# A four-layer kernel with post-norms: in the third layer 22 tiles of x are turned by the DMA as 16-bit planes, and ScalarE parts the planes of the first layer's pairs

## The chip, the cores and the metric

The kernel runs on one core of a Trainium2 chip. The metric is the time of one launch in microseconds on the device, as the median of several runs. The engines are TensorE (PE), VectorE (DVE), ScalarE (ACT), GpSimd (POOL) and SyncE (SP), which here only issues transfers.

## The reference

x has 4 batches of 1024 tokens with 1024 features. Four blocks follow one another, each with a residual and a layer norm:

```python
x = _layernorm(x + x @ (W0 * blockmask).T)                      # first layer
x = _layernorm(x + x @ W1.T + bias + lora_of_batch(x))          # second layer
x = _layernorm(x + mixer(x))     # to 128 features, 4 x (scan, MLP), back to 1024
x = _layernorm(x + x @ W.T + b + routed_lora(x))                # third layer
```

In the last line the router takes the mean of x over tokens 179 to 1022 of a batch, a softmax over 8 experts, and adds the experts' low-rank products with these weights. So the weights of a batch are only known when all its tiles have come out of the mixer.

## The kernel before

All work goes by tiles of 128 tokens, 32 for a layer, 8 for a batch. The counter s runs through the three dense layers: 0 to 31 the first, 32 to 63 (A_END, B_END) the second, 64 to 95 the third. A dense product has the weights as the wide operand and x, with the features on the partitions, as the narrow one. Both are split into a high part (fp32r) and the rest, and three matmuls of 128x512 are made for each of 8 chunks and 2 halves: lines 885 to 887, 48 matmuls a tile. ScalarE makes the high part of x (`split_x`, line 1370), VectorE the low one (line 1824).

**First layer.** Tiles 7 to 26 go in ten pairs (a, a+1), each by seven products of half size (A11, A12, S2, S3, S1, S4, A22, lines 964 to 966, 12 matmuls each). A11, S2 and S1 accumulate in bank 0, and ScalarE copies it out after each (`hold` 0, 1, 2, line 1391). The sums of x that S1 to S4 take are made by VectorE (`add_x`, lines 1872 to 1879). VectorE joins a bank with a held part into the rows of the output (`join`, line 1894): join 1 reads S3's bank and hold 2, and A22 must wait for it. The order of each engine is written out by hand. For pair p+1 the operands are made while pair p is multiplied.

A finished row is normalised in place by ScalarE (`normalise`, lines 1411 and 1414, after GpSimd's root, line 2625). The second layer needs it with the features on the partitions. In the first layer GpSimd therefore copies its lower and its upper 16 bits into two planes (`part_planes`, line 2636, one buffer), ScalarE's queue stores them (`send_planes`, line 1422), SyncE's queue reads them back with a transposing DMA (line 632), and GpSimd joins the planes to 32-bit words (`join_planes`, line 2643).

**Third layer.** Its input comes from the mixer's readout: for tile c of the mixer TensorE makes 6 matmuls (`read_out`), VectorE adds the residual and takes statistics (`residual`, lines 2231 to 2243), GpSimd the root (`root_c`, line 2685), ScalarE normalises in place (`normalise_c`, line 1553) and stores the tile to `x3` (line 1557). VectorE and GpSimd add it to the batch's total (`add_up`). Here these tiles are called mix tiles. They lie in three places (`cx`). The mix tiles of batch b+1 are made during the steps of batch b; tiles 8 and 9 before. C_STEP says in which: steps 0 to 3 of batches 1 and 2, two tiles each; the first of a step is added in that step, the second at the start of the next. After step 4 (SUM_STEP; 5 in batch 0) TensorE reduces the total (`reduce_total`), and in steps 6 and 7 it makes 16 weight parts for the next batch, with VectorE, ScalarE and GpSimd (`weight_lo`, line 2650); SyncE loads them.

x of step s is loaded as it is (`load_x`, line 639, two places), turned on TensorE at the start of step s-1 by 8 transposes (`turn_x`, line 897), and split from PSUM. SyncE's queue holds the loads of x, of the mixer's output, of the mix tiles and of the weights in one order, and a wait there holds back what stands behind it. The load of a mix tile (`load_c`, line 681) waits until the tile before it in its place has been stored and added up.

## Time and profile before

| | us |
|---|---|
| median of 3 runs | 1653.36 |
| lowest, highest | 1652.39, 1657.66 |
| the profiled execution | 1656.23 |
| its span, first to last instruction | 1654.3 |
| TensorE busy | 1614.8 (98%) |
| VectorE, ScalarE, GpSimd busy | 1175.0, 666.4, 618.5 |
| TensorE's granted clock, mean | 0.988 |

The profiled execution is 2.9 us above the median, 1.9 us of it lie outside its span. Matmuls overlap: one of 128x512 shows 0.39 us, but they start 0.227 us apart. The pairs run from 94 to 306 us, the second layer from 370 to 816 us, the mixer to about 1160 us, the third layer to the end.

### The profile page before, as it was taken

What the parts mean: (1) busy time and instruction counts of PE and PEld (TensorE: products, weight loads), DVE (VectorE), ACT (ScalarE), POOL (GpSimd) and SP (SyncE); (2) the same over time, 40 slices, a digit from 0 to 9 for tenths busy, and PEclk for the clock granted to TensorE, in tenths of its full rate; (3) what the DMA queues carried; (4) which work ended last, traced back from release to release, by engine and by line L of the source; (5) the groups of instructions that cost most, each with busy time, mean ns of one, the idle gap of its engine ahead of it and who ended that gap; (6) DMA issues with size and microseconds to landing.
All of it is one profiled execution on the core that took longest, in us unless ns stands there. A gap on an engine that the chain in (4) does not pass through costs nothing.

```text
span 1654.3 us, 22809 instructions
## 1 busy us (share of the span) xinstructions
PE 1614.8 (98%) x7734; PEld 1299.1 (79%) x7734; DVE 1175.0 (71%) x2150; ACT 666.4 (40%) x987; POOL 618.5 (37%) x507
## 2 busy tenths in 40 slices
PE   8999999999999999999999999999899999999998
PEld 7877777788888888888866666676788788888886
DVE  6978888566666666568878777778767776676633
ACT  3544443443333333323345555545433333343311
POOL 4323333353333323213577777762213222221200
PEclk9999999999999999999999999999899999999999
DMA  7233333555444444543140000003546555555321
GB/s 281 78 114 102 121 102 102 183 144 131 118 120 120 119 114 125 152 113 77 46 158 27 1 1 1 1 13 115 203 147 214 193 196 188 181 203 182 138 79 51
DMA packets 140195, 196.58 MB, mean 119 GB/s; under 512 B 75954, under 2 KB 84146, under 8 KB 139826
## 3 DMA queue, kind: packets, MB, share of 16 engines
q1 hardware_dynamic: 115250, 125.92, 26.3%
q10 hardware_dynamic: 24832, 69.22, 11.0%
q8 instruction: 63, 1.03, 0.3%
q14 instruction: 50, 0.41, 0.1%
HBM read 105.97 MB, written 72.35 MB: 108 GB/s over the span
## 4 chain that ended last, share of the span: by engine, by line
PE 78%; DVE 10%; issue 5%; ACT 3%; DMA 2%; POOL 1%; ACTq 0%; SPq 0%; DVEq 0%; POOLq 0%
PE ps L885 15%; PE ps L887 14%; PE ps L886 14%; PE ps L1131 7%; PE ps L1073 3%; PE ps L1031 2%; PE ps L1079 2%; PE ps L1123 2%; PE ps L964 2%; PE ps L1121 2%; PE ps L1122 2%; PE ps L897 2%; PE ps L966 2%; PE ps L965 2%; PE ps L1099 1%
## 5 line engine op out<-in xcount | busy, mean ns | idle before, releaser
L2625 POOL TENSOR_TENSOR rstd<-var_eps,minus_half 128x1 f32<-128x1 f32 x96 | 89.8, 936 | 556.9 <-DVE minus_mean L1909 556.9
L885 PE MATMUL ps<-wall_x,x_hi 128*128 128x512 f32 x688 | 273.8, 398 | 4.9 <-ACT wall_x L1476 2.1
L887 PE MATMUL ps<-wall_x,x_lo 128*128 128x512 f32 x688 | 268.9, 391 | 0.0
L886 PE MATMUL ps<-wall_x,x_hi 128*128 128x512 f32 x688 | 268.8, 391 | 0.0
L885 PE MATMUL ps<-wall_y,x_hi 128*128 128x512 f32 x512 | 201.9, 394 | 0.0
L886 PE MATMUL ps<-wall_y,x_hi 128*128 128x512 f32 x512 | 199.4, 389 | 0.0
L887 PE MATMUL ps<-wall_y,x_lo 128*128 128x512 f32 x512 | 199.4, 389 | 0.0
L885 PEld LDWEIGHTS ps<-wall_x,x_hi 128*128 128x128 f32 x688 | 129.6, 188 | 34.5 <-ACT wall_x L1476 4.4
L887 PEld LDWEIGHTS ps<-wall_x,x_lo 128*128 128x128 f32 x688 | 129.5, 188 | 27.8
L886 PEld LDWEIGHTS ps<-wall_x,x_hi 128*128 128x128 f32 x688 | 129.7, 189 | 25.2
L1841 DVE TENSOR_TENSOR row<-ps,bias 128x512 f32<-128x512 f32 x128 | 87.8, 686 | 86.8 <-PE ps L887 85.5
L1542 ACT ACTIVATE g<-ps,b 128x512 f32<-128x512 f32 x128 | 83.8, 679 | 123.8 <-PE ps L1123 123.3
L1131 PE MATMUL ps<-g,w 128*128 128x512 f32 x256 | 127.1, 619 | 0.0
L1844 DVE BATCH_NORM_STATS2 stats<-row 128x6 f32<-128x512 f32 x152 | 105.1, 694 | 26.2 <-ACT row L1404 21.8
L1414 ACT ACTIVATE row<-row,shift,rstd 128x1024 f32<-128x1024 f32 x96 | 119.5, 1245 | 3.2
L1411 ACT ACTIVATE shift<-minus_mean,rstd 128x1 f32<-128x1 f32 x96 | 28.0, 292 | 223.0 <-POOL rstd L2625 222.9
L887 PEld LDWEIGHTS ps<-wall_y,x_lo 128*128 128x128 f32 x512 | 96.1, 188 | 20.4
L886 PEld LDWEIGHTS ps<-wall_y,x_hi 128*128 128x128 f32 x512 | 96.2, 188 | 18.9
L885 PEld LDWEIGHTS ps<-wall_y,x_hi 128*128 128x128 f32 x512 | 96.2, 188 | 18.8
L2643 POOL COPY x_in<-x_planes 128x1024 uint16<-128x1024 uint16 x64 | 86.3, 1395 | 29.1 <-DMA x_planes<-x_scratch 26.1
L1370 ACT ACTIVATE x_hi<-ps 128x1024 fp32r<-128x1024 f32 x32 | 32.7, 1023 | 151.1 <-PE ps L897 148.1
L2636 POOL COPY planes_early<-row 128x1024 uint16<-128x1024 uint16 x54 | 65.9, 1249 | 61.2 <-ACT row L1414 48.1
(329 smaller groups left out, 3633.9 us busy)
## 6 DMA issues: line engine op xcount, KB each, us to landing
x_scratch<-row ACTq DMA_DIRECT2D x32, 512.0 KB, 2.7
x_in<-x_scratch SPq DMA_DIRECT2D x32, 512.0 KB, 4.0
out<-row ACTq DMA_DIRECT2D x32, 512.0 KB, 2.8
x_in<-in_x_t SPq DMA_DIRECT2D x29, 512.0 KB, 3.8
w_first<-in_w_t SPq DMA_DIRECT2D x56, 256.0 KB, 2.9
x_scratch<-planes_early ACTq DMA_DIRECT2D x27, 512.0 KB, 3.3
cx<-x_scratch SPq DMA_DIRECT2D x24, 512.0 KB, 4.3
x_scratch<-cx ACTq DMA_DIRECT2D x24, 512.0 KB, 3.6
```

What stands on the lines that cost most here:

```text
L885: pe.matmul(bank, hi[:, k], wall[:, k, 0, cols], start=(k == 0), stop=False)
L886: pe.matmul(bank, hi[:, k], wall[:, k, 1, cols], start=False, stop=False)
L887: return pe.matmul(bank, lo[:, k], wall[:, k, 0, cols], start=False, stop=(k == KC - 1))
L1073: last = pe.matmul(ps[:, bank, c:c + 1], squares[:, c * P:(c + 1) * P], mean_col[:], start=True, stop=True)
L1131: pe.matmul(ps[:, OUT], w2[:, FCH * (n // UNITS) + i], g[:, i], start=(i == 0), stop=(i == FCH - 1)).then_inc(o_done, 1)
L1414: act.activation(row[:, i], row[:, i], ACT.Identity, bias=shift[:, i:i + 1], scale=rstd[:, i:i + 1])\
L1542: act.activation(g[:, i], ps[:, F0 + i % 2], ACT.Silu, bias=of_layer(b1[:, :, i], n))\
L1841: dve.tensor_tensor(row[:, i, cols], ps[:, out_bank(s, half)], bias[:, cols], ALU.add)\
L1844: mark(dve.bn_stats(stats[:, i, half], row[:, i, cols]))
L2625: pool.tensor_tensor(rstd[:, i:i + 1], var_eps[:, i:i + 1], minus_half[:, 0:1], ALU.pow)\
L2636: pool.tensor_copy(planes[s >= S_END][:, part], halves[:, part]).then_inc(parted, 1)
L2643: pool.tensor_copy(halves[:, part], x_planes[:, part].rearrange("p k t -> p (k t)"))\
```

## The change

- **Third layer.** From mix tile 10 on (`C_PLANES`), that is from step 74 (`PLANES_FROM`), the tiles go by planes. ScalarE parts a normalised mix tile into two planes (`part_c`, 2 activations) and issues two stores instead of one. The planes go to two places that alternate (`c_planes`), one of them with its second half in a place of its own. SyncE issues two transposing DMAs for the step two ahead, instead of a plain load for the step three ahead. GpSimd joins them (`join_planes(s + 2)`, behind the roots and sums of the step), and x is split from SBUF. TensorE turns only tiles 64 to 73.
- **The places of mix tiles.** `load_c` waits until the tile before it is parted, not until it is stored.
- **Pairs.** The planes of tiles 7 to 24 and of tile 6 are parted by ScalarE, not GpSimd. ScalarE's order in a pair changes: parting of a-2, `normalise(a - 1)` and A12's high part come ahead of hold 1, the parting of a-1 behind it.

```diff
@@ turn_count, c_stores and new helpers
+C_PLANES = TPB + 2
+PLANES_FROM = B_END + C_PLANES
+def c_norm_count(c):
+    return c + 1 + 2 * max(0, c - C_PLANES)
@@ load_x
-                if s - 2 >= B_END:
+                if s > PLANES_FROM:
+                    sp.wait_ge(x_turned, turn_count(s - 1))
+                elif s - 2 >= B_END:
                     sp.wait_ge(x_turned, turn_count(s - 2))
...
-                    sp.wait_ge(c_stored[c_slot(c)], 16 * c_uses(c))
+                    sp.wait_ge(c_stored[c_slot(c)], c_stores(c))
+                    if s >= PLANES_FROM:
+                        for part in range(2):
+                            sp.dma_start_transpose(x_planes[:, part], x3_planes[c - C_PLANES, part])\
+                              .then_inc(x_loaded[0], 16)
+                        return
@@ load_c
-                    sp.wait_ge(c_stored[slot], 16 * c_uses(last))
+                    if last < C_PLANES:
+                        sp.wait_ge(c_stored[slot], c_stores(last))
+                    else:
+                        sp.wait_ge(c_normed, c_norm_count(last) + 2)
@@ SyncE, steps of the third layer
-                    load_x(s + 3)
+                    if s + 3 < PLANES_FROM:
+                        load_x(s + 3)
+                    if s + 2 >= PLANES_FROM:
+                        load_x(s + 2)
@@ TensorE, steps of the third layer
-                    if s + 1 < D_END:
+                    if s + 1 < PLANES_FROM:
                         turn_x(s + 1)
@@ ScalarE, new functions
+            def part_planes(s):
+                halves = row[:, s % 2].bitcast(U16).rearrange("p (f h) -> p h f", h=2)
+                act.wait_ge(normed, norm_count(s))
+                act.wait_ge(stored[(s - 1) % 2], 16 * ((s - 1) // 2 + 1))
+                for part in range(2):
+                    act.activation(planes[0][:, part], halves[:, part], ACT.Identity).then_inc(parted, 1)
+                send_planes(s)
+            def part_c(c):
+                act.wait_ge(c_normed, c_norm_count(c))
+                at_least(act, c_stored[c_slot(c)], c_stores(c) - 32)
+                if c >= C_PLANES + 2:
+                    act.wait_ge(c_stored[c_slot(c - 2)], c_stores(c - 2))
+                halves = c_place(c).bitcast(U16).rearrange("p (f h) -> p h f", h=2)
+                for part in range(2):
+                    act.activation(c_planes[c % 2][part][:], halves[:, part], ACT.Identity).then_inc(c_normed, 1)
+                act.wait_ge(c_normed, c_norm_count(c) + 2)
+                for part in range(2):
+                    act.dma_start(x3_planes[c - C_PLANES, part], c_planes[c % 2][part][:])\
+                       .then_inc(c_stored[c_slot(c)], 16)
@@ ScalarE, pairs
                 if p > 0:
-                    send_planes(a - 2)
-                hold(p, 1)
+                    part_planes(a - 2)
                 normalise(a - 1)
                 if more:
                     op_hi(p + 1, A12)
                 else:
                     split_x(S_END)
+                hold(p, 1)
+                part_planes(a - 1)
...
-                send_planes(a - 1)
@@ ScalarE, steps of the third layer
-                    for i in C_STEP[b].get(j - 1, ()):
-                        normalise_c(c + i)
+                    late = C_STEP[b].get(j - 1, ())
+                    if late:
+                        normalise_c(c + late[0])
+                        part_c(c + late[0])
+                        normalise_c(c + late[1])
+                        part_c(c + late[1])
@@ GpSimd, pairs
-                if p > 0:
-                    part_planes(a - 2)
                 root(a - 1)
-                part_planes(a - 1)
@@ GpSimd, steps of the third layer
+                    if PLANES_FROM <= s + 2 < D_END:
+                        join_planes(s + 2)
                     for i in PART_STEP[b].get(j, ()):
```

**ScalarE in a pair of the first layer**, before. `held` is hold 0 and then hold 1; `x_in_125` is tile a+1, `x_in_126` the next pair's first tile:

```order
L1384 ACTIVATE x_hi<-x_in_125 128x512
L1391 ACTIVATE held<-ps 128x512
L1384 ACTIVATE x_hi<-x_in_126 128x512
L1422 DMA x_scratch<-planes_early 128x2x1024
L1391 ACTIVATE held<-ps 128x512
L1411 ACTIVATE shift<-minus_mean,rstd 128x1
L1414 ACTIVATE row<-row,shift,rstd 128x1024
L1384 ACTIVATE x_hi<-x_in_126 128x512
L1384 ACTIVATE sum_hi<-x_sum 128x512 x2
```

And with the change:

```order
L1417 ACTIVATE x_hi<-x_in_125 128x512
L1424 ACTIVATE held<-ps 128x512
L1417 ACTIVATE x_hi<-x_in_126 128x512
L1458 ACTIVATE planes_early<-row 128x1024 x2
L1463 DMA x_scratch<-planes_early 128x2x1024
L1444 ACTIVATE shift<-minus_mean,rstd 128x1
L1447 ACTIVATE row<-row,shift,rstd 128x1024
L1417 ACTIVATE x_hi<-x_in_126 128x512
L1424 ACTIVATE held<-ps 128x512
L1458 ACTIVATE planes_early<-row 128x1024 x2
L1463 DMA x_scratch<-planes_early 128x2x1024
L1417 ACTIVATE sum_hi<-x_sum 128x512 x2
```

Two partings have come in, and A12's high part (the second `x_in_126`) stands ahead of the second `held` instead of behind it.

**SyncE around the start of step 3 of batch 1**, before: two mix tiles, then x, then the mixer's output of the next mix tile:

```order
L681 DMA cx_146<-x_scratch 128x1024
L681 DMA cx_147<-x_scratch 128x1024
L639 DMA x_in_126<-x_scratch 128x1024
L691 DMA cz<-z_hi_scratch 128x128
L691 DMA cz<-z_lo_scratch 128x128
```

And with the change:

```order
L711 DMA cx_146<-x_scratch 128x1024
L711 DMA cx_147<-x_scratch 128x1024
L663 DMA_TRANSPOSE x_planes<-x_planes 128x8x128 x2
L721 DMA cz<-z_hi_scratch 128x128
L721 DMA cz<-z_lo_scratch 128x128
```

The two transposes stand where the load of x stood, but for the step after the next.

**GpSimd in step 2 of batch 1**, before, from the root of the last step's row:

```order
L2625 TENSOR_TENSOR rstd<-var_eps,minus_half 128x1
L2703 TENSOR_TENSOR total<-cx_147,total 128x512
L2685 TENSOR_TENSOR c_rstd<-c_var_eps,minus_half 128x1
L2703 TENSOR_TENSOR total<-cx_145,total 128x512
L2685 TENSOR_TENSOR c_rstd<-c_var_eps,minus_half 128x1
```

And with the change:

```order
L2684 TENSOR_TENSOR rstd<-var_eps,minus_half 128x1
L2765 TENSOR_TENSOR total<-cx_147,total 128x512
L2747 TENSOR_TENSOR c_rstd<-c_var_eps,minus_half 128x1
L2765 TENSOR_TENSOR total<-cx_145,total 128x512
L2747 TENSOR_TENSOR c_rstd<-c_var_eps,minus_half 128x1
L2704 COPY x_in_126<-x_planes 128x1024 x2
```

The join has come in behind the root of the step's first new mix tile.

## Rows read from the trace of the kernel before

**Rows 1.** The page, part 1: busy time of the engines.
```profile
PE 1614.8 (98%) x7734; PEld 1299.1 (79%) x7734; DVE 1175.0 (71%) x2150; ACT 666.4 (40%) x987; POOL 618.5 (37%) x507
```

**Rows 2.** TensorE's waits, whole span: us in total, times, longest.
```profile
PE ps L964 <- DVE row L1894: 12.1, 9, 2.3
```

**Rows 3.** Stretches: us, busy PE, PEld, DVE, ACT, POOL, clock, DMA share, GB/s.
```profile
94.00:306.00 212.00, 198.26 (x858) 160.62 (x857) 171.75 (x394) 91.03 (x149) 66.12 (x62) 0.99 0.33 108
410.00:700.00 290.00, 289.86 (x1485) 246.54 (x1484) 182.94 (x294) 105.91 (x159) 85.40 (x63) 1.00 0.48 125
1331.00:1436.00 105.00, 105.00 (x515) 87.39 (x514) 76.25 (x152) 40.87 (x56) 26.00 (x27) 1.00 0.59 198
```

**Rows 4.** Timeline of ScalarE in a pair: start us, us, instruction, idle before.
```profile
167.54 0.60 ACT L1391 ACTIVATE held<-ps 128x512 f32<-128x512 f32 x1 [4.01 <-PE ps L966]
...
169.50 0.61 ACT L1384 ACTIVATE x_hi<-x_in 128x512 fp32r<-128x512 f32 x1
```

**Rows 5.** Timeline of VectorE in the same pair.
```profile
170.15 1.09 DVE L1851 TENSOR_TENSOR x_lo<-x_in,x_hi 128x512 fp32r<-128x512 f32 x1 [2.68 <-ACT x_hi L1384]
171.16 1.52 DVE L1872 TENSOR_TENSOR x_sum<-x_in 128x512 f32<-128x512 f32 x1
...
174.53 1.28 DVE L1851 TENSOR_TENSOR sum_lo<-x_sum,sum_hi 128x512 fp32r<-128x512 f32 x2
175.74 0.68 DVE L1894 TENSOR_TENSOR row<-ps,held 128x512 f32<-128x512 f32 x1
```

**Rows 6.** Timeline of GpSimd in the same pair: a root, two copies of planes.
```profile
165.56 0.98 POOL L2625 TENSOR_TENSOR rstd<-var_eps,minus_half 128x1 f32<-128x1 f32 x1 [0.22 <-DVE minus_mean L1909]
169.66 2.48 POOL L2636 COPY planes_early<-row 128x1024 uint16<-128x1024 uint16 x2 [3.12 <-ACT row L1414]
```

**Rows 7.** Timeline of TensorE from S4 to A22 of that pair.
```profile
175.27 0.39 PE L966 MATMUL ps<-wall_x,sum_lo 128*128 128x512 f32 x1
176.57 0.47 PE L964 MATMUL ps<-wall_y,x_hi 128*128 128x512 f32 x1 [0.91 <-DVE row L1894]
```

**Rows 8.** The first layer's planes, 94 to 306 us: duration ns min/median/max.
```profile
L1422 ACTq DMA_DIRECT2D x_scratch<-planes_early x20: 378/378/429, 97.8 to 298.6; - x20
...
DMA to landing us min/median/max: 2.8/3.3/6.8
```

**Rows 9.** TensorE at a step's start; then its transposes, grouped, 1330 to 1637.
```profile
1359.06 0.39 PE L1157 MATMUL ps<-wout_hi,cz 128*128 128x512 f32 x1
...
1360.39 0.40 PE L886 MATMUL ps<-wall_y,x_hi 128*128 128x512 f32 x1
...
L897 PE MATMUL ps<-ident,x_in 128*128 128x128 f32 x176 | 22.8, 273 | 0.0
```

**Rows 10.** Timeline of ScalarE in step 3 of batch 1.
```profile
1360.36 1.03 ACT L1370 ACTIVATE x_hi<-ps 128x1024 fp32r<-128x1024 f32 x1 [5.98 <-PE ps L897]
...
1363.65 1.25 ACT L1553 ACTIVATE cx<-cx,c_shift,c_rstd 128x1024 f32<-128x1024 f32 x1
```

**Rows 11.** Timeline of VectorE in that step, and in a weight step.
```profile
1362.56 0.68 DVE L2231 TENSOR_TENSOR cx<-ps,cx 128x512 f32<-128x512 f32 x1
...
1371.13 0.15 DVE L2243 TENSOR_SCALAR c_minus_mean<-c_mean_var 128x1 f32<-128x1 f32 x1
...
1430.83 0.69 DVE L1933 TENSOR_TENSOR w_in<-ps,w_in 128x512 f32<-128x512 f32 x1 [0.67 <-PE ps L989]
```

**Rows 12.** Planes in the second layer: SyncE's issues, GpSimd's join, the landing.
```profile
514.45 2.67 SPq L632 DMA_TRANSPOSE x_planes<-x_scratch  x2
...
520.67 2.61 POOL L2643 COPY x_in<-x_planes 128x1024 uint16<-128x1024 uint16 x2 [2.24 <-DMA x_planes<-x_scratch]
...
DMA to landing us min/median/max: 3.0/3.9/5.6
```

**Rows 13.** Timeline of GpSimd in step 3, and in a weight step.
```profile
1371.30 0.99 POOL L2685 TENSOR_TENSOR c_rstd<-c_var_eps,minus_half 128x1 f32<-128x1 f32 x1 [1.03 <-DVE c_minus_mean L2243]
...
1424.68 1.29 POOL L2650 TENSOR_TENSOR wall_x<-w_in,wall_x 128x512 fp32r<-128x512 f32 x1 [3.31 <-ACT wall_x L1476]
```

More of the change, by code:

```diff
@@ L145, in x_loads @@
         return even + 2 * (s - A_END + 1)
+    if s >= PLANES_FROM:
+        return x_loads(PLANES_FROM - 2) + 2 * (s - PLANES_FROM + 1)
     return (odd if s % 2 else even + 2 * TILES) + (s - B_END) // 2 + 1
@@ L157, in turn_count, with by_dma @@
 def turn_count(s):
-    return 2 * (s - A_END + 1) if s < B_END else 2 * TILES + s - B_END + 1
+    return 2 * (s - A_END + 1) if s < B_END else 2 * TILES + s - B_END + 1 + max(0, s - PLANES_FROM + 1)
+def by_dma(s):
+    return A_END <= s < B_END or s >= PLANES_FROM
+def c_norm_count(c):
+    return c + 1 + 2 * max(0, c - C_PLANES)
 def before_in_slot(s):
@@ L215, in c_uses, with c_stores @@
     return (2 if i % 3 == 2 else 3) * b + i // 3 + 1
+def c_stores(c):
+    return 16 * (c_uses(c) + sum(c_slot(i) == c_slot(c) for i in range(C_PLANES, c + 1)))
 def c_before(c):
@@ L248, in build @@
     x2 = scratch("x2_scratch", (TILES, P, D))
-    x3 = scratch("x3_scratch", (TILES, P, D))
+    x3 = scratch("x3_scratch", (C_PLANES, P, D))
+    x3_planes = scratch("x3_planes", (TILES - C_PLANES, 2, P, D), U16)
     h0 = scratch("h0_scratch", (P, TOKENS))
@@ L383, in build @@
     bias_rows = at("bias_rows", R, [P, D])
+    c_planes = [[at(f"c_planes{i}_{part}", offset, [P, D], U16) for part, offset in enumerate(places)]
+                for i, places in enumerate(((R + 20480, R + 22528), (FACTOR + 12288, W)))]
     cz = at("cz", R + 24576, [P, 2, 2, P], F32R)
@@ L661, in load_b @@
                     c = TPB * batch + 5
-                    sp.wait_ge(c_stored[2], 16 * c_uses(c))
+                    sp.wait_ge(c_stored[2], c_stores(c))
                     sp.wait_ge(totalled[0], c_sums(c))
@@ L1360, in split_x @@
                     act.wait_ge(x_turned, turn_count(s))
-                    src = x_in[1][:] if s < B_END else ps_x
+                    src = x_in[1][:] if by_dma(s) else ps_x
                 if s == B_END:
@@ L1554, in normalise_c @@
                    .then_inc(c_normed, 1)
-                act.wait_ge(c_normed, c + 1)
-                at_least(act, c_stored[c_slot(c)], 16 * (c_uses(c) - 1))
-                act.dma_start(x3[c], place).then_inc(c_stored[c_slot(c)], 16)
+                if c < C_PLANES:
+                    act.wait_ge(c_normed, c_norm_count(c))
+                    at_least(act, c_stored[c_slot(c)], 16 * (c_uses(c) - 1))
+                    act.dma_start(x3[c], place).then_inc(c_stored[c_slot(c)], 16)
+            def part_c(c):
+                act.wait_ge(c_normed, c_norm_count(c))
+                at_least(act, c_stored[c_slot(c)], c_stores(c) - 32)
[8 more added lines that the diff above has]
+                       .then_inc(c_stored[c_slot(c)], 16)
             def router_exp(batch):
@@ L1814, in split_x @@
             def split_x(s):
-                src = x_first[:, s] if s < FIRST else x_in[s % 2 if s < A_END else 1][:] if s < B_END else ps_x
+                src = x_first[:, s] if s < FIRST else x_in[s % 2 if s < A_END else 1][:] if s < A_END or by_dma(s) else ps_x
                 hi, lo = [flat(t) for t in x_parts(s)]
@@ L2255, in add_up @@
                     return
-                dve.wait_ge(c_normed, c + 1)
+                dve.wait_ge(c_normed, c_norm_count(c))
                 if i == 1:
@@ L2641, in join_planes @@
                 halves = x_in[1][:].bitcast(U16).rearrange("p (f h) -> p h f", h=2)
+                if s == PLANES_FROM:
+                    pool.wait_ge(x_turned, turn_count(s - 1))
                 for part in range(2):
@@ L2683, in root_c @@
                 pool.wait_ge(c_ve_ready, 2 * c + 1)
-                at_least(pool, c_normed, c - 1)
+                if c >= 2:
+                    pool.wait_ge(c_normed, c_norm_count(c - 2))
                 pool.tensor_tensor(c_rstd[:, i:i + 1], c_var_eps[:, i:i + 1], minus_half[:, 0:1], ALU.pow)\
@@ L2692, in add_up @@
                     return
-                pool.wait_ge(c_normed, c + 1)
+                pool.wait_ge(c_normed, c_norm_count(c))
                 if i == 1:
```

1 line of the change is left out of this document (added).

## The prediction

> **What bounds the kernel now.** I read the page first: TensorE is busy for 98% of the span [rows 1]. So time is only won where TensorE idles, or by taking work from it. The table of TensorE's waits names one large wait, 12.1 us in 9 pieces of up to 2.3 us, all before a matmul of line 964 and all ended by the addition of line 1894 [rows 2]: once in nine of the ten pairs of the first layer. In the third layer TensorE is busy without a gap (105.00 us of 105.00) and the granted clock is 1.00 [rows 3]; there the reader is to look at what it does: 8 transposes in each step [rows 9].
>
> Where the pair's wait comes from is seen in the timelines of the pair at 167 us. ScalarE evacuates S2 (line 1391, 167.54), normalises tile a-1, and only then makes A12's high part (169.50) [rows 4]. VectorE waits for that: low part at 170.15, four sums, two more low parts, and the join of S3 at 175.74 [rows 5]. TensorE's last matmul of S4 starts at 175.27, A22's first at 176.57 [rows 7]: 1.30 us where 0.23 is the usual distance. Two of VectorE's operations are long (1.09, 1.52 against about 0.65 in [rows 5]) while GpSimd copies planes (169.66 to 172.14) [rows 6].
>
> **The change, part by part.**
>
> *1. Pairs: ScalarE parts the planes, hold 1 comes later.* A pair is 7 products of 12 matmuls at 0.227 us: 19.1 us without a wait. I count from T, A22's start. From the rows, A11 is done at T+5.7, S2 at T+11.1, S1 at T+16.6, and A22 may start at T+19.1. A parting is two activations 128x1024; no ScalarE row has 16-bit operands. Bounds are the two nearest rows of that size, 1.03 (a plain copy) and 1.25 (with shift and scale) [rows 10]; I take 1.03, the row without pointers, so 2.0 us a tile, plus an issue of about 0.4. ScalarE's order then gives: normalise a-2 at T+3.5 to 5.0 (behind VectorE's join of S4, statistics and aggregate, some 2.2 us, and a root of 0.98 [rows 6]), A22, hold 0 and A11 to T+6.9, parting to 8.9, issue to 9.3, normalise a-1 to 10.9, A12 to 11.5, hold 1 to 12.1. S1 starts at T+13.7, so hold 1 isn't late. The second parting must wait for the first tile's store: it lands 3.3 us after its issue (6.8 at most) [rows 8], so T+12.7 to 14.7, issue to 15.2; S2 and S3 high to 16.4; hold 2 to 17.2. VectorE, without GpSimd's copies beside it, has A12's low part at 12.2, sums to 14.9, low parts to 17.1, the join to 18.0. That is 1.1 us before A22: the wait goes, and next late is S1's own evacuation.
>
> The waits are 12.1 us, and each costs some 0.16 more between starts (1.30 - 0.23 = 1.07 against the 0.91 named in [rows 7]): 13.5 us. What stays: in the pair after the longest set-up work on VectorE (pair 1), hold 1 comes about 0.7 us after S1 could start, 0.3 in two others; and in the last pair the first half of the adapter's rows is evacuated only after the parting, 0.5 us later than now. 13.5 - 1.8 = **11.7 won**. With 1.25 a part, 0.8 us of the 1.1 us cover is gone, and the wait does not return. GpSimd's copies have no one behind them in the pairs; their end is worth nothing more.
>
> The Trainium skill (ScalarE: Activation LUTs, What ACT_TABLE_LOAD costs) gives 186 ns + 0.833 ns an element with immediate operands, whatever the function: 1.04 us here, the same sum. It names fp32 and bf16, not 16-bit integers.
>
> *2. 22 tiles are not turned by TensorE.* 8 transposes stand between the last matmul before them (1359.06) and the second after them (1360.39): 1.33 - 2 x 0.227 = 0.88 us a tile [rows 9]. The stretch shows 176 of them, 22 tiles: 22 x 0.88 = **19.4 won** at most, since nothing else covers them.
>
> *3. What comes in their place.* GpSimd joins two planes: 2.61 us a tile [rows 12]. It is idle enough (26.00 of 105.00 us) [rows 3]; 22 joins are 57 us beside other work. But the join stands behind the root of the step's first mix tile, and the split of x waits for it. For steps with two mix tiles (60 matmuls, 13.6 us) I follow the ring from one split to the next. On VectorE: split at 1360.36 [rows 10], the statistics of the first new tile at 1371.13 [rows 11], root 0.99 from 1371.30 [rows 13], join 2.61: 14.6 us. On SyncE: split, mix tile normalised at 1364.90 [rows 10] (+4.5), parted +6.5, then the load into its place, behind which both transposes stand in SyncE's queue: +6.9. In the second layer the first issue to the copy's start is 6.2 us (514.45 to 520.67), 2.24 of them spent waiting for the transfer; landing is 3.0 to 5.6, median 3.9 [rows 12]. Ready at +11.8 (if 4.9) to +13.1, join: 14.5 to 15.8 us. I take 15.2 for the ring, 1.6 more than a step, in three steps of batch 1 and again of batch 2. The first split is 0.2 us before the step's start in batch 1, whose step 0 still has 0.9 us of transposes, and 0.4 after it in batch 2. In the third step it is 3.0 late; the addition of the second mix tile's halves ends 2.9 and 4.2 after it (from 1360.36 and the 1362.56 of [rows 11]), TensorE asks at +5.4 and +6.1: 1.1 us lost. In the fourth, where the batch's sums must be complete before the reduction (48 matmuls, +10.9), the split is 3.5 late and the last sum ends 10.4 after it: 3.0 lost. Batch 1 loses 4.1, batch 2 5.0: **9.1 lost**, 5.5 with a ring of 14.6 and 13.1 with 15.8.
>
> *4. Weight steps.* At step 7 of batches 1 and 2 the transposes stand behind the weights in SyncE's queue, and GpSimd joins before its low parts (one at 1424.68 now [rows 13]); it would come 4 us later, and so a weight load with it. VectorE's sum of that part (1430.83 [rows 11]) comes about 3 us later; TensorE has the next part's product at about that time: 0 to 1 us a batch, 1.0 in all.
>
> *5. No cost.* ScalarE's 22 partings of mix tiles (45 us) lie in idle time (40.87 of 105.00 busy). The steps of batch 3 have 10.9 us and a ring of 2.6 + 6.2: covered. The DMA's busy share: 0.48 at 125 GB/s with transposes, 0.59 at 198 without [rows 3]; so transposing costs 0.48 - 0.59 x 125/198 = 0.11, and the third layer goes to 0.70. No queue is full.
>
> Beside GpSimd's copies only VectorE's operations with both inputs in SBUF are long [rows 5, 6]; most of a C step reads PSUM. The Trainium skill (SBUF — State Buffer, Who interferes with whom) has the shared port pair as an exclusive lock. By a full block, two copies cost VectorE up to 2.6 us a step, which would be the stalls of rival 3. The rows speak for less: 0.4 and 0.85 us, on such operations alone.
>
> **Sum.** Against the profiled execution: 1656.2 - 11.7 - 19.4 + 9.1 + 1.0 = 1635.2 us. The median of the runs is 2.9 us lower (1653.36): **1632**. The half-speed stretch near 136 us, after the long wait of pair 1, is left in; without it 1.6 us less.
>
> **Rivals.**
> 1. *No ring.* Transposes land early and roots take 0.55, not 0.99; the splits stay in step. For it: the median landing of 3.9. 1653.4 - 13.5 - 19.4 - 1.6 = 1619.
> 2. *The pairs don't win.* The change doesn't do there what it says: ScalarE's longer queue (store wait, second parting) holds S1's or S3's evacuation back by the 1.1 us that the path had. Against: ScalarE is busy 91 of 212 us [rows 3]. 1632 + 11.7 = 1644.
> 3. *The transfers are slow in the third layer,* at a share of 0.70: 3 us more to landing. Ring 18.2; per batch the fourth step's sums end at -0.2 + 54.6 + 10.4 = 64.8 against 51.7: 13 lost, 26 in both, 17 more than forecast; batch 3, ring near 11.8 on 10.9, some 1. About 1650: no measurable change. For it: the step carries a mix load, two plane stores and the output at that time.
> 4. *Slower: parts of 2.1 us on ScalarE,* twice the row of that size, because 16-bit halves at 4-byte distance are read in two passes. Then the pair's second parting ends at T+18.2, hold 2 at 20.4, the join at 21.1; with 0.6 at S1 2.1 us a pair, 21 us against the 13.5 of now: +7.5. Ring 17.3: 25 us lost in batches 1 and 2. 1653.4 + 7.5 - 19.4 + 25 + 1 = 1668. It decides from some 1.7 us a part, and nothing in the rows excludes a 16-bit form that slow; all ScalarE rows of 1024 columns are near 1.0 or 1.25.
>
> **How the numbers follow.** Forecast 0.62, its own range 1626 to 1638; rival 1 0.13, rival 2 0.10, rival 3 0.10, rival 4 0.05. The range 1619 to 1645 holds the forecast and rivals 1 and 2 and leaves out the others. A measurement here tells 0.3%, 5 us, from no change: the bounds are 1648.4 and 1658.3. Faster: 0.62 + 0.13 + 0.10, and a little of rival 3: 0.86; within 0.09; slower 0.05.
>
> **What would show it.** Line 964's wait for the join gone or under 2 us; activations of planes near 1.03 us; no transposes of x after step 73; in batches 1 and 2 the split of x starting later with each step, TensorE waiting for the mix tile's addition in the third and at the reduction in the fourth, together near 9 us; GpSimd's joins ended by the DMA, not by a root. Wrong would be: waits of TensorE for the split itself, a part over 1.3 us, landings over 6 us, or losses in batch 3.

## The result, and the profile of the changed kernel

The changed kernel is not faster. Measured against the kernel before on the same chip its ratio was 1.0061 (95% interval 1.0035 to 1.0088): median 1666.21 us, 4 runs from 1661.71 to 1666.90, against 1655.17. A second, larger set (the run both_halves, below: 10 runs of the changed kernel, 19 of the kernel before) gave 1.0015 (1.0001 to 1.0029), 1658.98 against 1656.5. The two sets differ by more than their intervals; both lie at or above 1. The forecast was 1632.

The profiled execution took 1661.71 us with a span of 1659.8. First the page, part 1, which answers [rows 1]:

```profile
PE 1605.1 (97%) x7558; PEld 1284.6 (77%) x7558; DVE 1159.8 (70%) x2150; ACT 748.5 (45%) x1069; POOL 642.2 (39%) x513
```

TensorE has 176 instructions fewer and 9.7 us less work than in [rows 1], and the span is 5.5 us longer: so it idles more. The table of TensorE's waits (us in total, times, longest), which answers [rows 2], says where:

```profile
PE ps L1198 <- DVE total L2327: 9.3, 2, 6.0
PE ps L1188 <- DVE cx L2290: 7.4, 5, 3.5
PE ps L1032 <- ACT b_rows L1479: 3.7, 1, 3.7
PE ps L997 <- DVE sum_lo L1910: 2.5, 1, 2.5
...
PE ps L997 <- DVE row L1953: 0.5, 2, 0.3
```

The last of these is the old wait for the join in the pairs, 12.1 us in [rows 2]: 0.5 us of it are left. The first two are new and lie in the third layer: the reduction (line 1198) waits for the sum over the batch, the mix tile's read-out (line 1188) for the addition of the tile before. The third lies in the last pair and was 0.9 us before. The stretches, which answer [rows 3], and behind them four short ones (us, busy PE, PEld, DVE, ACT, POOL, clock, DMA share, GB/s):

```profile
94.00:306.00 212.00, 204.55 (x885) 167.23 (x884) 158.63 (x404) 132.58 (x195) 27.48 (x30) 0.98 0.36 115
1331.00:1436.00 105.00, 96.50 (x417) 77.32 (x416) 69.19 (x135) 49.26 (x63) 44.73 (x39) 0.95 0.62 183
1361.10:1364.50 3.40, 3.40 (x10) 2.65 (x8) 3.30 (x8) 2.37 (x4) 2.23 (x2) 0.50 0.21 20
1384.90:1391.70 6.80, 6.80 (x24) 5.83 (x24) 2.38 (x6) 2.48 (x3) 3.11 (x3) 0.50 1.01 303
1470.30:1477.10 6.80, 6.01 (x14) 4.66 (x15) 6.59 (x14) 5.24 (x7) 2.24 (x2) 0.50 0.36 123
1511.20:1521.40 10.20, 8.16 (x27) 7.21 (x28) 4.43 (x9) 4.93 (x6) 3.80 (x4) 0.50 0.79 259
```

In the same 105 us of the third layer TensorE was busy for 105.00 before and is for 96.50 now. In the last four the granted clock is 0.50, that is 1.2 GHz instead of 2.4, and matmuls of 512 columns start 0.43 us apart instead of 0.23. TensorE had waited ahead of them: starts are 3.9 us apart at 1355.6, and it idles 3.3 us from 1381.0, before the reduction. Of the 27.2 us it is busy for 24.4, so I estimate their cost at half of that, 12.2 us. In the kernel before the clock is 1.00 from 1320 to 1640.

How long each step of the third layer takes can be read from the starts of its first products. The table has the steps in which something changes besides the transposes (us; the last three columns are experiments):

| step | before | after | waits_kept | z_behind | join_first |
|---|---|---|---|---|---|
| batch 1, step 2 | 14.5 | 14.9 | 13.6 | 13.6 | 13.6 |
| step 3 | 14.5 | 19.6 | 14.6 | 13.7 | 13.6 |
| step 4 (reduction) | 13.5 | 17.3 | 17.2 | 16.3 | 13.9 |
| step 5 | 12.9 | 14.2 | 13.8 | 14.1 | 13.7 |
| batch 2, step 2 | 14.5 | 19.6 | 15.2 | 13.6 | 13.6 |
| step 3 | 14.5 | 14.0 | 14.7 | 13.6 | 13.6 |
| step 4 (reduction) | 13.5 | 20.4 | 15.9 | 15.9 | 14.0 |
| step 5 | 12.9 | 14.3 | 14.6 | 14.5 | 13.7 |

All other steps from batch 1 on are 0.88 to 0.91 us shorter than before (the first 0.80), batch 3's too (11.8 to 10.9), but for the weight steps (step 7: 17.2 to 17.6 and 17.9) and the last two. I use one measure for all kernels: the time from the first product of tile 66 to the end of the span. It was 433.0 us before. Less the 19.4 us of the transposes it would be 413.6, and what a kernel has over that is its **loss**. The changed kernel has 446.9, so it loses 33.3 us; of these I had forecast 10.1.

Why is seen on SyncE, ScalarE and GpSimd in batch 1. First the table of SyncE's waits from 1320 to 1372, then its timeline:

```profile
SPq L707 <- DVE total L2330: 16.6, 2, 9.6
SPq L719 <- PE ps L1190: 6.2, 2, 5.5
SPq L710 <- ACT c_planes L1608: 6.0, 1, 6.0
```

```profile
1329.09 0.32 SPq L711 DMA_DIRECT2D cx<-x_scratch  x1
1329.50 4.31 SPq L663 DMA_TRANSPOSE x_planes<-x_planes  x2
...
1345.19 0.32 SPq L711 DMA_DIRECT2D cx<-x_scratch  x1
1345.61 4.66 SPq L663 DMA_TRANSPOSE x_planes<-x_planes  x2
```

SyncE stands for 22.6 of 52 us ahead of a mix tile's load (lines 707, 710), whose place must first be parted and added up, and 0.1 us after that load come the transposes. The standing alone is not new. The same table of the kernel before has 19.7 us of it (then for the place to be stored, line 680):

```profile
SPq L677 <- DVE total L2271: 10.6, 2, 5.5
SPq L680 <- DMA x_scratch<-cx: 9.1, 4, 7.1
```

What is new is what stands behind it in the queue. The transposes take 4.31 and 4.66 us to issue, not the 2.67 of [rows 12]. The timelines of ScalarE (the parting ends at 1345.1, the load goes at 1345.19) and GpSimd:

```profile
1338.52 1.06 ACT L1403 ACTIVATE x_hi<-x_in 128x1024 fp32r<-128x1024 f32 x1 [4.90 <-POOL x_in L2704]
...
1341.84 1.24 ACT L1594 ACTIVATE cx<-cx,c_shift,c_rstd 128x1024 f32<-128x1024 f32 x1
1343.11 2.01 ACT L1608 ACTIVATE c_planes<-cx 128x1024 uint16<-128x1024 uint16 x2
...
1356.46 1.06 ACT L1403 ACTIVATE x_hi<-x_in 128x1024 fp32r<-128x1024 f32 x1 [6.74 <-POOL x_in L2704]
```

```profile
1353.85 2.58 POOL L2704 COPY x_in<-x_planes 128x1024 uint16<-128x1024 uint16 x2 [3.14 <-DMA x_planes<-x_planes]
```

This is the ring of the prediction, on the path that it named: split, norm, parting, load, transposes, join, split. But GpSimd waits 3.14 us for the transfer, and from split to split it is 17.9 us. The four splits of batch 1 start at 1321.69, 1338.52, 1356.46 and 1373.55: 16.8, 17.9 and 17.1 us apart where I took 15.2.

### The profile page after: what moved, and what is told of

It reads as the page before. It is cut to its first block, busy times and chain, and to the rows that moved or that the text cites. A ratio compares the mean times of both kernels' runs of the same rounds, so it can differ in the third digit from the quotient of the medians.

```text
span 1659.8 us, 22589 instructions
## 1 busy us (share of the span) xinstructions
PE 1605.1 (97%) x7558; PEld 1284.6 (77%) x7558; DVE 1159.8 (70%) x2150; ACT 748.5 (45%) x1069; POOL 642.2 (39%) x513
## 3 DMA queue, kind: packets, MB, share of 16 engines
q10 hardware_dynamic: 28000, 69.22, 10.9%
## 4 chain that ended last, share of the span: by engine, by line
PE 69%; DVE 10%; issue 6%; ACT 5%; POOL 4%; DMA 3%; SPq 1%; ACTq 1%; POOLq 0%; DVEq 0%
PE ps L918 12%; PE ps L919 12%; PE ps L920 12%; PE ps L1164 6%; PE ps L1106 3%; PE ps L997 3%; PE ps L998 3%; PE ps L999 3%; PE ps L1064 2%; PE ps L1112 2%; PE ps L1156 2%; PE ps L1155 2%; PE ps L1154 2%; PE ps L1132 1%; DVE c_stats L2292 1%
## 5 line engine op out<-in xcount | busy, mean ns | idle before, releaser
L2684 POOL TENSOR_TENSOR rstd<-var_eps,minus_half 128x1 f32<-128x1 f32 x96 | 100.9, 1051 | 584.1 <-DVE minus_mean L1968 584.1
L2704 POOL COPY x_in<-x_planes 128x1024 uint16<-128x1024 uint16 x108 | 143.3, 1374 | 60.9 <-DMA x_planes<-x_planes 29.3
L918 PEld LDWEIGHTS ps<-wall_y,x_hi 128*128 128x128 f32 x512 | 97.2, 190 | 19.7
L1403 ACT ACTIVATE x_hi<-x_in 128x1024 fp32r<-128x1024 f32 x63 | 66.7, 1058 | 89.9 <-POOL x_in L2704 50.7
L1883 DVE TENSOR_TENSOR x_lo<-x_in,x_hi 128x1024 fp32r<-128x1024 f32 x63 | 77.6, 1231 | 33.6 <-ACT x_hi L1403 33.1
```

Source lines behind the costliest of these rows:

```text
L918: pe.matmul(bank, hi[:, k], wall[:, k, 0, cols], start=(k == 0), stop=False)
L1403: act.activation(flat(x_parts(s)[0]), src, ACT.Identity).then_inc(hi_ready, 1)
L1883: dve.tensor_tensor(lo, src, hi.bitcast(F32), ALU.subtract).then_inc(lo_ready, 1)
L2684: pool.tensor_tensor(rstd[:, i:i + 1], var_eps[:, i:i + 1], minus_half[:, 0:1], ALU.pow)\
L2704: pool.tensor_copy(halves[:, part], x_planes[:, part].rearrange("p k t -> p (k t)"))\
```

## The experiments

All ratios are against the kernel before, timed on the same chip beside the kernels of each group. Its median was 1656.62 us beside pairs_only, third_only, loads_behind and batch3_only; 1655.0 beside pick_first, z_behind, join_first and join_first_pick; 1655.22 beside waits_kept and norms_first; 1656.5 beside both_halves and after_pick. A **loss** is always read from the one profiled execution of a kernel, a time from the median of its runs.

**The halves alone.** pairs_only is the kernel before with ScalarE parting the pairs' planes; third_only is the changed kernel with GpSimd parting them as before.

> The kernel before with the pairs' half of the change alone: ScalarE parts the pairs' planes, the third layer stays as before. Theory: the nine waits for the join are gone (12.1 us in the trace before), a new wait of 3.7 us stands ahead of the last pair's pick, with a stretch at the lower clock behind it; I read about 8 us of gain at 1184 us in the trace of the changed kernel, so about 1647 us against 1655, ratio 0.995. Rival: the first pair's longer wait (2.9 us for sum_lo, 1.2 before) belongs to the change too, and other runs lose more there: 1652 or more. If the pairs are the cause of the whole miss: over 1660.

> The changed kernel with the pairs' half taken back: GpSimd parts the pairs' planes as before, the third layer keeps its 22 tiles by planes. Theory: in the third layer 18.9 us are saved on TensorE and about 33 us are lost to waits and to the lower clock behind them, so 14 us over the kernel before: 1669 to 1675 us, ratio about 1.010. Rival: the losses depend on luck of the transfers in one trace and are about the 10 us that I took before: then 1646 us.

Measured: pairs_only 1643.69 us, ratio 0.9928 (0.9910 to 0.9946); third_only 1671.63 us, 1.0086 (1.0065 to 1.0107). By these ratios the pairs win 12 us; the third layer, which was to win 9.3, costs 14. In third_only's trace its loss is 31.7 us. In pairs_only's trace ScalarE and TensorE in the last pair:

```profile
281.70 2.00 ACT L1425 ACTIVATE planes_early<-row 128x1024 uint16<-128x1024 uint16 x2 [3.77 <-DMA x_scratch<-planes_early]
283.74 0.38 ACTq L1430 DMA_DIRECT2D x_scratch<-planes_early  x1
284.16 0.60 ACT L1446 ACTIVATE b_rows<-ps 128x512 fp32r<-128x512 f32 x1 [0.46 <-ACT planes_early L1425]
```

```profile
284.81 0.50 PE L999 MATMUL ps<-lora,pick 128*128 128x512 f32 x1 [4.79 <-ACT b_rows L1446]
```

ScalarE stands 3.77 us for the landing of the first tile's planes, with the picked rows queued behind it, and TensorE waits for those (0.9 us in the kernel before).

**The last pair.** The call for the rows is moved ahead of the parting:

```
                 hold(p, 1)
+                if not more:
+                    take_b(0, 0)
                 part_planes(a - 1)
                 if more:
                     op_hi(p + 1, S2)
                     op_hi(p + 1, S3)
-                else:
-                    take_b(0, 0)
```

> The pairs' half alone, as in the run pairs_only, with one call moved: in the last pair ScalarE copies out the first half of the picked rows ahead of the parting of the tile before, not behind it. Theory: in the run pairs_only ScalarE stood 3.7 us for the landing of the planes' store before (issued at 274.2, landed by 281.7) with the picked rows queued behind it, TensorE waited 5.2 us and then ran about 4 us at the lower clock; with the call moved about 4 of the 5.2 us and the 1.8 us of lower clock are gone: 5 to 6 us less than pairs_only, about 1638 us. Rival: another wait of the last pair ends at the same time, and no more than 2 us are won: 1642.

Measured: 1640.69 us, 0.9902 (0.9879 to 0.9925). The rows are copied at 276.83, still within the products, and the wait is gone; from tile 6's second half to tile 27's first product it is 199.7 us where pairs_only has 206.6 and the kernel before 215.0. I had expected 5 to 6 us less than pairs_only. The medians show only 3 us of these 7 (the ratios 4): a wait of 1.8 us for the first weights appears right behind the pairs, and in the shared stretch from there to the third layer this trace is the slower. The same move on two other kernels (below) gave 7.9 and 7.6 us.

**SyncE's order.** In loads_behind the mix loads that wait for something late stand a step later:

```
-C_LOAD = ({2: (4, 5), 3: (6, 7)},) + 2 * ({0: (3,), 1: (4, 5), 2: (6, 7)},) + ({},)
+C_LOAD = ({2: (4, 5), 3: (6, 7)},) + 2 * ({1: (3, 4), 2: (5, 6), 3: (7,)},) + ({},)
```

> The changed kernel with SyncE's order in the third layer changed alone: of the mix tiles' loads those that wait for a part or a norm of the same step (tiles 3, 5 and 7 of a batch) stand one step later, behind the two transposes. The work is the same. Theory (the ring goes through SyncE's queue): the transposes no longer wait for the late mix tile's parts, GpSimd's join no longer waits for them, and of the 33 us lost in batches 1 and 2 at most 8 are left: 1637 to 1644 us. Rival A (ScalarE's four parts a step, or VectorE behind them, are simply too long for a step): the losses stay, 1660 to 1667. Rival B (the transposes are slow, 4.3 to 4.7 us instead of 2.7, and delay wherever they stand): about half of it stays, 1650 to 1656.

Measured: 1645.36 us, 0.9934 (0.9919 to 0.9949); loss 18.4 us. That is between my figure and rival B's: 15 us of the changed kernel's loss are back, 18 remain. SyncE, and VectorE in step 2 of batch 1, show why:

```profile
1334.89 0.97 SPq L721 DMA_DIRECT2D cz<-z_lo_scratch  x1
1336.04 0.82 SPq L711 DMA_DIRECT2D cx<-x_scratch  x2
1336.96 4.99 SPq L663 DMA_TRANSPOSE x_planes<-x_planes  x2
```

```profile
1340.38 0.69 DVE L2290 TENSOR_TENSOR cx<-ps,cx 128x512 f32<-128x512 f32 x1 [3.67 <-DMA cx<-x_scratch]
```

Two mix loads still stand right ahead of the transposes, held up by a z load that waits for the end of the step, and now tile 3 comes too late as well.

**A smaller piece of the layer.** In batch3_only the constant `C_PLANES` is `3 * TPB` and `part_c` is called for those tiles alone, so only the last eight tiles go by planes.

> The changed kernel with the last batch's eight tiles alone by planes: batches 1 and 2 of the third layer turn theirs on TensorE as before. The parts of these eight mix tiles are still made by ScalarE in the C steps of batch 2, but no transposes and joins run in those steps. Theory (ring): no losses but for about 1 us at the weights, 8 x 0.88 = 7.0 us saved, and the pairs' 8 us: 1640 us. Rival A (ScalarE's parts themselves delay the C steps): batch 2 loses its 18 us as in the changed kernel, so about 1657 us.

Measured: 1640.76 us, 0.9901 (0.9885 to 0.9917). Batch 2 up to its step 5, with ScalarE's four parts in a step but without transposes and joins, as a stretch:

```profile
1427.00:1512.00 85.00, 85.00 (x425) 70.69 (x423) 61.01 (x126) 45.26 (x54) 18.40 (x21) 1.00 0.59 192
```

TensorE is busy for all of it. Rival A falls: by themselves the parts cost nothing. The layer is 5.5 us shorter than before (427.5), 7.0 less 1.5 lost at the weights.

**The order in full, and the join ahead.** z_behind places each load that waits for the end of its step behind the next step's transposes, tile 3 ahead of z4:

```
-Z_LOAD = ({2: (4, 5), 3: (6, 7)},) + 2 * ({0: (2, 3), 1: (4, 5), 2: (6, 7)},) + ({},)
-C_LOAD = ({2: (4, 5), 3: (6, 7)},) + 2 * ({0: (3,), 1: (4, 5), 2: (6, 7)},) + ({},)
+MIX_LOAD = ({2: "z4 z5 c4 c5", 3: "z6 z7 c6 c7"},) + 2 * ({0: "z2", 1: "z3 c3 z4 c4",
+            2: "z5 c5 z6 c6", 3: "z7 c7"},) + ({},)
...
```

Here z and c stand for the loads of the mixer's output and of the mix tile; the cut leaves out the loop that goes through this list.

join_first is z_behind with GpSimd's order changed:

```
+                    if PLANES_FROM <= s + 2 < D_END:
+                        join_planes(s + 2)
                     for i in C_STEP[b].get(j, ())[:1]:
                         root_c(c + i)
-                    if PLANES_FROM <= s + 2 < D_END:
-                        join_planes(s + 2)
```

join_first_pick is join_first with pick_first's move.

> The changed kernel with SyncE's order changed further than in the run loads_behind: every load of the third layer that waits for something of the end of its step (the second of two z loads and the mix tile behind it) stands behind the next step's transposes, and tile 3 stands ahead of z4. Theory (the ring goes through SyncE's queue; and the transposes are slow only where a mix tile's load stands right ahead of them, 4.4 to 5.8 us against 2.5): the transposes take 2.5 to 2.7 us in all steps, VectorE no longer waits for tile 3's landing (4.0 us in loads_behind), and of the 18 us that loads_behind still lost at most 10 are left: about 1637 us against its 1645. Rival A (ScalarE and VectorE with the four parts and the joins are too full): no change, 1643 to 1646. Rival B (slow transposes by the stores of ScalarE's queue): they still take 4 us.

> As z_behind, and GpSimd's join stands ahead of the root of the step's first mix tile, which waits for TensorE's read-out in the middle of the step. Theory: in loads_behind the transposes of step 3 had landed by about 1344 and the join began at 1349.9, behind that root; with the join ahead x_hi starts within its own step and the losses at the reduction fall too: 2 to 4 us less than z_behind, 1633 to 1636. Rival: the join was not on the path, since the planes are needed a step later: within 1 us of z_behind. Or the join now delays the root, the norm and the reduction: slower by 2 us or more.

> As join_first with pick_first's move in the last pair. The two act in stretches that are 1000 us apart and should add: join_first less 5 to 6 us, 1628 to 1631.

Measured: z_behind 1640.82 us, 0.9909 (0.9886 to 0.9931), loss 14.4; join_first 1638.93 us, 0.9895 (0.9877 to 0.9913), loss 9.0; join_first_pick 1631.03 us, 0.9850 (0.9824 to 0.9875), loss 8.6. SyncE's waits of z_behind, from 1320 to 1372:

```profile
SPq L662 <- POOL x_in L2701: 15.9, 4, 7.5
SPq L706 <- DVE total L2327: 7.9, 3, 3.8
```

At the transposes SyncE now waits for the join that frees their place, which is what must be waited for; they issue in 2.6 us but for one pair (4.55 at 1334.58), and the splits are 14.0, 15.1 and 14.6 us apart. My figure for z_behind was 3.8 us too low, because I took all of the rest for SyncE's; the second part of the rest was GpSimd's order, seen in its timeline in step 2 (z_behind, then join_first):

```profile
1346.11 1.01 POOL L2744 TENSOR_TENSOR c_rstd<-c_var_eps,minus_half 128x1 f32<-128x1 f32 x1 [0.64 <-DVE c_minus_mean L2299]
1347.08 2.60 POOL L2701 COPY x_in<-x_planes 128x1024 uint16<-128x1024 uint16 x2
```

```profile
1348.71 3.05 POOL L2701 COPY x_in<-x_planes 128x1024 uint16<-128x1024 uint16 x2
1351.70 0.54 POOL L2744 TENSOR_TENSOR c_rstd<-c_var_eps,minus_half 128x1 f32<-128x1 f32 x1
```

With the join ahead no step loses anything but the reduction's, the one behind it and those of weights, and the two waits at the reduction fall from 4.5 to 2.2 us. The root behind it comes later and delays no one: ScalarE's waits for such roots are 2.0 us in either (1310 to 1370). The median of join_first is only 1.9 us below that of z_behind, less than the 2 to 4 that I expected and within the noise of the two ratios; the gain of 5.4 us is read from the two traces' losses, and the trace of join_first_pick has the same small loss, 8.6.

**The slow transposes by themselves.** In waits_kept SyncE keeps every wait where the change has it; only the issue of the last mix load of a step (and of the last at a batch's end) is put behind the transposes. `wait_c` and `send_c` are the two parts of `load_c`:

```
                         load_x(s + 2)
+                    for i in waited:
+                        send_c(i)
+                    waited.clear()
...
-                    for i in C_LOAD[b].get(j, ()):
+                    for i in C_LOAD[b].get(j, ())[:None if b == 0 else -1]:
                         load_c(c + i)
+                    for i in C_LOAD[b].get(j, ())[-1:] if b > 0 else ():
+                        wait_c(c + i)
+                        waited.append(c + i)
...
-                        load_c(c + TPB + 2)
+                        wait_c(c + TPB + 2)
+                        waited.append(c + TPB + 2)
```

> The changed kernel, in which SyncE still waits for the last mix tile of a step where it did, ahead of the transposes, but issues that tile's load behind them and no longer ahead. So the ring stays closed through SyncE's queue, and only the load that stood right ahead of the transposes is gone from there. Theory (two terms: the wait makes the ring, the load ahead makes the transposes take 4.4 to 5.8 us instead of 2.5): the transposes take 2.5 us at all steps, the ring falls from 16.8 to 17.9 us by about 2 us to 15 to 15.8, and the third layer loses some 20 us instead of 32: 1652 to 1656. Rival A (the transposes are slow by ScalarE's stores or by the traffic): they still take over 4 us, and the time stays at 1662 to 1667. Rival B (the slow transposes are the whole loss): losses as in z_behind, 1641.

Measured: 1643.71 us, 0.9930 (0.9912 to 0.9947), loss 18.3. SyncE, ScalarE (two splits) and TensorE's waits from 1307:

```profile
1342.17 2.84 SPq L663 DMA_TRANSPOSE x_planes<-x_planes  x2
```

```profile
1335.50 1.06 ACT L1418 ACTIVATE x_hi<-x_in 128x1024 fp32r<-128x1024 f32 x1 [3.45 <-POOL x_in L2719]
...
1350.29 1.06 ACT L1418 ACTIVATE x_hi<-x_in 128x1024 fp32r<-128x1024 f32 x1 [3.62 <-POOL x_in L2719]
```

```profile
PE ps L1213 <- DVE total L2342: 5.4, 2, 2.8
PE ps L1203 <- DVE cx L2305: 1.9, 5, 0.8
```

The four pairs of transposes of batch 1's C steps issue in 2.6 to 2.8 us, and the ring is 15.4, 14.8 and 14.8 us: the 15.2 of the prediction. The landing changes with it (line 663, 1320 to about 1370, us min/median/max; after, then waits_kept):

```profile
DMA to landing us min/median/max: 3.5/5.6/6.6
```

```profile
DMA to landing us min/median/max: 3.4/4.0/4.4
```

Rival A falls; the traffic is the same. Half of rival B holds: the slow transposes are 15 of the 33.3 us (12 of the 30.7 in the second trace of the change, below), and 18.3 remain without them. The time is lower than I expected for this run, 1643.7 and not 1652 to 1656, since I had taken the medians of the first set of the changed kernel for its level. It lies near rival B's 1641, but that was the time of z_behind, which itself still loses 14.4 us; so the time does not speak for rival B in full.

**A miss.** norms_first is join_first_pick with ScalarE's order of a C step turned from norm, parts, norm, parts into norm, norm, parts, parts.

> As join_first_pick, with ScalarE's order in the C steps changed: the norm of the second late tile stands ahead of the parts of the first, so that the mix's sum over the batch is ready 2.1 us earlier. Theory: the wait of 1.5 us that TensorE still has at each of two reductions goes, and the stretch of about 3.6 us at half the clock behind it (0.14 us more for each of some 9 products), so 3 to 5 us less than join_first_pick's 1631: about 1627. Rival: the first tile's parts come 1.5 us later and SyncE's wait for them, with the transposes behind it, takes the place: 1631 or more.

Measured: 1636.67 us, 0.9882 (0.9861 to 0.9903), loss 14.3 against join_first_pick's 8.6. The intervals of the two ratios overlap by a little, so it is the trace that shows the loss. ScalarE in step 4:

```profile
1366.12 0.29 ACT L1592 ACTIVATE c_shift<-c_minus_mean,c_rstd 128x1 f32<-128x1 f32 x1 [2.42 <-POOL c_rstd L2748]
```

The second norm has no root yet, and ScalarE stands 2.4 us for it, in which it made the first tile's parts before. Those, the load behind them and the transposes all come later: the rival of that text.

**Both halves again.**

> The changed kernel itself, once more. Its halves alone gave 0.9928 (pairs) and 1.0086 (third layer) of the kernel before; their product is 1.0013, 1657.4 us, but the changed kernel was measured at 1.0061. Theory A (the halves are independent, they lie 1000 us apart, and the difference lies between sets of runs): a median between 1657 and 1663. Theory B (with the pairs' half the third layer loses more): 1665 or more again, and in the trace a third layer some 5 us longer than the 445.3 us of third_only (from the first product of tile 66 to the end).

> The changed kernel with the one call of the last pair moved, as in pick_first: the picked rows are copied out ahead of the parting. Nothing of the third layer differs. From the positions behind the pairs in seven traces without the move (203.9 to 209.1 us from the first pair to the next product) and three with it (199.7 to 203.0) I expect 5 us less than the changed kernel of the same call, so about 1656 to 1660. Rival: the third layer's losses swallow it: equal to the changed kernel.

Measured: both_halves 1658.98 us, 1.0015 (1.0001 to 1.0029), loss 30.7; after_pick 1651.41 us, 0.9970 (0.9955 to 0.9986). The product of the two halves' ratios, 1.0013, is what the larger set shows: they add. after_pick lies 7.6 us under both_halves, where I had expected 5. Why the first set of the changed kernel lay 0.5% higher stays open. Its profiled execution can't tell: at 1661.71 us it was the fastest of its four, and near the level of the larger set.

## Why the prediction was wrong, step by step

| term of the sum | predicted | measured |
|---|---|---|
| pairs | -11.7 | -12 by the ratio of pairs_only, -8.4 in the pairs' own stretch of the traces |
| 22 tiles not turned by TensorE | -19.4 (0.88 each) | 0.80 in one step and 0.88 to 0.91 in eleven; the other ten hold losses and can't be read |
| a part on ScalarE | 1.03 | 1.04 to 1.06 |
| ring in C steps of batches 1 and 2 | +9.1 | 30.5 (33.3 less the weights) |
| weight steps | +1.0 | 2.8 |

*Pairs: right in size, and partly by luck.* The second parting's wait for the first store was in the working, and so was the picked rows' place behind it, but I priced that at 0.5 us with a landing of 3.3 us. In the last pair of pairs_only the next parting began 7.5 us after the store's issue (274.19 to 281.70), where [rows 8] gives 6.8 as the longest landing, and TensorE waited 4.8 (3.7 in the changed kernel). Behind that wait the clock is at its lower level for 3.4 us (285.2 in pairs_only), where the kernel before had such a stretch near 136 us. Against this, the 1.3 us that I left to late evacuations of S1 in three pairs did not appear: the table of waits names none, and the waits for the join are 0.5 us together. That doesn't make up for the 3.9 us more in the last pair. From tile 6's second half to tile 27's first product the traces show 215.0 us before and 206.6 in pairs_only, 8.4 won (10.7 from third_only, 219.0, to both_halves, 208.3). The rest of the 12 us lies in the stretch from tile 27 to tile 66, where the two kernels don't differ: 917.4 us before, 913.7 in pairs_only, up to 921.2 in the other traces.

*The step that failed is the ring's size, by the term for the transposes.* Its path, its first and worst places (the mix tile's addition, then the reduction) and its cause, a queue in which the transposes stand behind the mix load, were as written. I costed the transposes with a row of the second layer, 2.67 us [rows 12], where no mix load stands ahead of them. That term was 4.3 to 4.7 us here, from the first issue to the copy's start it took up to 8.2 us where I had at most 6.2, and the ring was 16.8 to 17.9 instead of 15.2. Since a ring's excess over the step is paid anew each step, 1.6 to 2.7 us more of it cost 15 us in two batches. waits_kept is the check on the rest: with a ring of 14.8 to 15.4, TensorE waits 7.3 us for additions and reductions, where the forecast had 9.1 (16.7 in the changed kernel).

*What was not in the sum:* the lower clock, which I put at nothing for the new waits, though I knew of such a stretch near 136 us in the base. In waits_kept it has two stretches, at the two reductions, with TensorE busy throughout:

```profile
1376.10:1382.90 6.80, 6.80 (x24) 6.10 (x25) 2.83 (x7) 2.88 (x4) 1.51 (x2) 0.50 1.00 237
1499.00:1505.80 6.80, 6.80 (x32) 5.18 (x32) 1.73 (x5) 2.48 (x3) 3.13 (x3) 0.50 0.99 309
```

At half the clock they cost some 6.8 us, against the 12.2 estimated for the changed kernel. So the 30.5 us divide like this: waits_kept, whose ring has the size that I forecast, loses 15.8 of them (18.3 less 2.5 at the weights). The 14.7 us between the two are the slow transposes, in longer waits and in more of the lower clock. Of the 15.8, 7.3 are waits, where I had 9.1; 6.8 are the lower clock, where I had nothing; what the last 1.7 are stays open.

*Rivals.* Rival 3 had the right kind of fault, slow transfers in the third layer and a ring of 18.2, but put it down to the load on the DMA and gave it 0.10. Its 28 us of loss (26, 1 in batch 3 and 1 at the weights) stand against 33.3 measured, where batch 3 lost nothing, and with it the time would have been 1650. The DMA's share in the stretch of [rows 3] is 0.62, not the 0.70 that I had worked out. Rival 4 (parts of 2.1 us) is excluded by the 1.04 us. The Trainium skill (ScalarE: Activation LUTs, What ACT_TABLE_LOAD costs) has figures from which I estimate 1.04 us for this shape, and the trace agrees, with 16-bit integers at a distance of 4 bytes too. Of my own list of what would be wrong, landings over 6 us came true (up to 6.6 in batch 1's C steps, up to 7.3 in batch 2's).

*The range* reached to 1645. I had widened the ring by the landing alone and given the issue of 2.67 us no bound. The trace of the kernel before had one, in the second layer (410 to 700 us, one transpose, ns min/median/max):

```profile
L632 SPq DMA_TRANSPOSE x_planes<-x_scratch x42: 1242/1296/2927, 418.2 to 690.6; - x42
```

With 2.9 us for the second transpose the ring's upper end would have been some 1.6 us higher, 17.4, and its loss some 22 us (between the 13.1 at 15.8 and the 26 at 18.2). That is 13 us over the forecast's 9.1, so 1645, and that still lies under both measured medians, since the lower clock is not in it.

## What to carry to other kernels

Where one queue carries both the loads that free-up buffers and the transfers that the next step waits for, look at what stands ahead of the latter, and cost the transfer from a row where the same kind of instruction stands ahead. A path that closes on itself from step to step must be summed with its longest values, because each microsecond over the step is paid in every step. A new wait of TensorE needs a second term, for the lower clock that can follow it. The change itself is good once the order is right: with SyncE's loads and GpSimd's join reordered and one call moved in the last pair, the same 22 tiles by planes give 0.985 of the kernel before.

## What the runs showed of the hardware

A DMA transpose of 128x1024 16-bit values takes SyncE 1.24 to 1.30 us to issue in most places; a plain load takes 0.32 to 0.5. Where a mix tile's load ended within 0.4 us ahead of the pair, the second transpose took 2.7 to 4.7 us, in the changed kernel and in loads_behind. Behind weight loads, even 0.1 us behind, the pair took 2.6 to 3.3 (1421.30 and 1562.38 in the changed kernel), and it took 2.6 as well at 2.5 and 7.5 us behind a mix load (z_behind, 1349.71 and 1364.28). Between these the distance alone doesn't tell: 1.6 us behind such a load the pair took 4.55 us in one batch and 2.87 in the next (z_behind, 1334.58 and 1453.54), 0.8 us behind another 2.66 (join_first, 1351.79). Two mix loads and four z loads at a batch's end slow it too (5.45 us at 1427.59 in waits_kept). That the load ahead, and not ScalarE's stores, makes the difference in the C steps is shown by waits_kept, where the stores stand as in the change; by what mechanism stays open.

VectorE beside GpSimd's copies behaved otherwise than I had argued. In join_first_pick, VectorE and GpSimd in step 3:

```profile
1353.95 1.48 DVE L2327 TENSOR_TENSOR total<-cx,total 128x512 f32<-128x512 f32 x1
```

```profile
1353.57 3.05 POOL L2701 COPY x_in<-x_planes 128x1024 uint16<-128x1024 uint16 x2
```

The addition, with both inputs in SBUF, takes 0.68 us without a copy beside it (1343.52 in loads_behind). Here it began 0.4 us into the first copy, of 1.36 us, and ended 0.5 us after that copy's end; the two copies took 3.05 us instead of 2.6. The first copy has its usual length (1.35 in z_behind), the second took 1.8. So each seems to wait for the end of the other's instruction. The Trainium skill (SBUF — State Buffer, Who interferes with whom) calls the port pair an exclusive lock, and the trace agrees: the price is the rest of the running instruction, 0.8 us here, and not the 2.6 us of two whole copies that I had held against it.

The granted clock of TensorE fell behind short waits too: in join_first_pick TensorE waits 1.1 us ahead of batch 1's reduction, whose products have one column each, and from 1370.1 on the clock is 0.50 for 3.4 us.
